# A decoder layer on one core: the order of loads, weights and first queries in the prologue

## The chip, the cores and the metric

One core of a Trainium2 chip. The metric is the device time of one execution in microseconds, the median of several. TensorE, VectorE, ScalarE and GpSimd each run their own instruction stream and wait for each other by semaphores; SP issues DMAs. All DMAs of the core run on its 16 DMA engines.

## The reference

One decoder layer over x of 4 x 512 tokens, 512 features, in float32:

```
x = x + attention(layernorm(x))        # norm again with g_norm, q = xn @ Wq (16 heads of 128),
                                       # k, v = xn @ Wkv (one head shared by all), q and k l2-normalised,
                                       # softmax(4 q . 4 k) @ v, @ Wout, layernorm with g_out
x = x + experts(layernorm(x), ids)     # silu(h @ Wg.T) * (h @ Wu.T) @ Wd.T, one of 4 experts by token id,
                                       # all three weights are ctx
x = x + bitlinear ffn(layernorm(x))    # weights rounded to -1, 0, 1, inputs to 8 bits, gelu between
```

## The kernel before, in words

Nearly every matrix product is done as three 16-bit products (`split_products`): each operand is a high part and a low part (the rest), and high x high, high x low and low x high are summed in PSUM. High parts are made by ScalarE, low parts by VectorE. A batch of x has four tiles of 128 tokens.

The prologue, batch 0:
- SP loads x 0, the norm weights `gn` (512 values spread over 128 partitions, four bytes each), x 1 to 3, Wkv (512 KB), the token ids `idi` (2048 four-byte pieces) and block 0 of Wq (1 MB, four heads; there are four blocks). Then `turn_x` transposes the four tiles by DMA, each after its low part (`x_lo`), and Wq blocks 1 and 2 and two pieces of Wout follow.
- VectorE waits for GpSimd's constants (`consts`), takes statistics (`input_stats`), normalises (`input_norm`), and makes low parts (`input_low`). GpSimd makes the power -0.5 (`input_rstd`). ScalarE makes high parts (`input_high`). `gws` is the norm weight times 64; it scales the rows of Wkv and Wq when their high and low parts are made (`query_weight`, per block and chunk of 128 features, one chunk 512 columns; `query_weight_high` is the high part on VectorE, used for block 1).
- TensorE runs 33 filler products (`busy_small`) once two low parts are there, then `keys_values` 0 and 1 (tiles 0, 1 and 2, 3: 24 products of 256 columns each), two small products for the routing of tokens to experts, query blocks 0 to 5, twelve fillers, and the loop over heads.
- A query block `queries(u)` is one tile of 128 tokens by four heads: 12 products of 512 columns. Its banks are `S` for u = 0 to 3, `QB` or `OUTB` after that. After it ScalarE takes squares (`query_squares`), GpSimd the power (`query_norm`), ScalarE the high part (`query_high`), VectorE the low part (`query_low`), and SP transposes the result (`turn_q`). Scores of heads 0 to 3 need all four blocks 0 to 3.
- VectorE does the routing (`routing_counts`, `routing_places`) between the weights of block 0 and the low parts of the keys.

The loop over 64 steps (four batches of 16 heads), step g on TensorE: `scores(g)` (12 products of 512 columns), `values(g - 1)` (48 products of 128 or 129 columns), from head 16 on `outputs`, and `queries(g + 6)`. ScalarE makes the exponentials of g in two halves, VectorE casts them and subtracts (`probabilities`); these low parts (`p_lo`) release `values(g)`. GpSimd turns a piece of Wout per step (`wout_parts`). In steps 11 and 12 the keys of the next batch are done too. Block 3 of Wq is turned into parts in steps 1 to 5, x of the next batch in steps 0 to 9.

The experts and the ffn follow; the change doesn't touch them.

## Time and profile before

| | |
|---|---|
| median of 3 runs | 955.84 us (954.51 to 956.09) |
| the profiled execution | 953.94 us |
| its span | 952.1 us, 19241 instructions |
| TensorE busy | 919.0 us, 97% |
| VectorE busy | 701.6 us, 74% |
| ScalarE busy | 616.5 us, 65% |
| GpSimd busy | 328.1 us, 34% |
| queue of SP (and ScalarE) | 117.25 MB, 56.2% of 16 DMA engines |

The span is the time on the device between the first and the last recorded instruction; the execution's own time has 1.8 us more around it. A busy TensorE is a row of products one behind the other: a product's own duration is longer than its distance to the next. Line numbers are those of the kernel before.

### The profile page before, as it was taken

Reading aid. Unit: us, or ns where it says so; the run is one execution under the profiler, and the core shown is the slowest. Engines: PE = TensorE matmul, PEld = TensorE weight load, DVE = VectorE, ACT = ScalarE, POOL = GpSimd, SP = SyncE. Lnnn points to the kernel's source line nnn. Section 1 sums busy time; section 2 is a strip of 40 time slices with the busy share of each in tenths; the row PEclk is TensorE's granted clock in tenths of the full one; section 3 lists DMA queues with packets and bytes.
Section 4 is the critical chain, followed back from the end, with each engine's and each line's share of the span. In section 5 each row is a group of like instructions: output and inputs, shape, how many; then the busy total and the mean of one; then the engine's idle time right before and its main releaser. Section 6 shows DMA issues by size and latency. Waiting matters only on the chain.

```text
span 952.1 us, 19241 instructions
## 1 busy us (share of the span) xinstructions
PE 919.0 (97%) x6635; PEld 522.8 (55%) x6635; DVE 701.6 (74%) x1540; ACT 616.5 (65%) x1573; POOL 328.1 (34%) x454
## 2 busy tenths in 40 slices
PE   4999999999999999999999999999997999999995
PEld 3466676655656556655666555656543444444442
DVE  6799978787786767787576766688564468877784
ACT  4877777767776756766667666765302269988672
POOL 4578867223332314323233313221141012322222
PEclk9999999999999999999999999999999999999998
DMA  9747547577867654554535444447985998544352
GB/s 243 176 90 136 122 101 119 137 196 170 211 167 156 156 135 110 112 134 112 127 81 120 100 112 101 116 106 177 206 210 134 192 191 166 119 96 97 86 135 73
DMA packets 303599, 131.60 MB, mean 138 GB/s; under 512 B 273168, under 2 KB 277776, under 8 KB 303504
## 3 DMA queue, kind: packets, MB, share of 16 engines
q1 hardware_dynamic: 299504, 117.25, 56.2%
q0 software_dynamic: 4000, 13.13, 3.9%
q8 instruction: 54, 0.88, 0.4%
q14 instruction: 41, 0.34, 0.1%
HBM read 42.76 MB, written 21.25 MB: 67 GB/s over the span
## 4 chain that ended last, share of the span: by engine, by line
PE 84%; DVE 5%; DMA 4%; ACT 2%; issue 2%; POOL 1%; SPq 1%; DVEq 0%; ACTq 0%; POOLq 0%
PE S L260 8%; PE S L258 8%; PE S L259 8%; PE O L635 6%; PE O L633 6%; PE O L637 6%; PE QB L258 6%; PE QB L259 6%; PE QB L260 6%; PE OUTB L259 5%; PE OUTB L258 5%; PE OUTB L260 5%; PE S L762 4%; PE OUTB L796 4%; DMA P<-QTOKR 2%
## 5 line engine op out<-in xcount | busy, mean ns | idle before, releaser
L633 PE MATMUL O<-V,P 128*128 128x129 f16 x1024 | 179.0, 219 | 1.6 <-DVE P L1255 1.4
L635 PE MATMUL O<-V,P 128*128 128x128 f16 x1024 | 179.1, 221 | 0.0
L637 PE MATMUL O<-V,P 128*128 128x129 f16 x1024 | 178.9, 218 | 0.0
L1253 DVE CAST P<-P 128x1024 bf16<-128x1024 f32 x128 | 93.2, 728 | 111.9 <-ACT P L915 111.8
L1255 DVE TENSOR_TENSOR P<-P 128x1024 f16<-128x1024 f32 x128 | 160.7, 1256 | 4.4
L915 ACT ACTIVATE P<-S,cst 128x1024 f32<-128x1024 f32 x128 | 142.5, 1114 | 29.1 <-PE S L260 27.4
L1609 POOL TENSOR_SCALAR qst<-qs 128x4 f32<-128x4 f32 x64 | 14.4, 225 | 344.1 <-ACT junk L898 344.1
L898 ACT ACTIVATE junk<-QB 128x128 bf16<-128x128 f32 x208 | 54.6, 277 | 102.1 <-PE QB L260 102.1
L926 ACT ACTIVATE OTOK<-O,rd 128x128 f16<-128x128 f32 x256 | 80.6, 376 | 43.1 <-DVE rd L1260 40.4
L633 PEld LDWEIGHTS O<-V,P 128*128 128x128 bf16 x1024 | 98.5, 96 | 9.7 <-DVE P L1255 2.5
L635 PEld LDWEIGHTS O<-V,P 128*128 128x128 bf16 x1024 | 99.2, 97 | 7.2
L637 PEld LDWEIGHTS O<-V,P 128*128 128x128 f16 x1024 | 100.8, 98 | 0.0
L258 PE MATMUL S<-XQA,KT 128*128 128x512 f16 x256 | 97.0, 379 | 0.3 <-DMA XQA<-P 0.3
L260 PE MATMUL S<-XQA,KT 128*128 128x512 f16 x256 | 97.0, 379 | 0.0
L259 PE MATMUL S<-XQA,KT 128*128 128x512 f16 x256 | 97.0, 379 | 0.0
L258 PE MATMUL QB<-WQA,XQA 128*128 128x512 f16 x208 | 78.8, 379 | 0.7 <-DVE QTOKR L1243 0.7
L259 PE MATMUL QB<-WQA,XQA 128*128 128x512 f16 x208 | 78.8, 379 | 0.0
L260 PE MATMUL QB<-WQA,XQA 128*128 128x512 f16 x208 | 78.8, 379 | 0.0
L1610 POOL TENSOR_TENSOR rn<-qst,half 128x4 f32<-128x4 f32 x64 | 71.3, 1115 | 5.3
L259 PE MATMUL OUTB<-WOA,OTA 128*128 128x512 f16 x192 | 72.8, 379 | 0.0
L260 PE MATMUL OUTB<-WOA,OTA 128*128 128x512 f16 x192 | 72.8, 379 | 0.0
L258 PE MATMUL OUTB<-WOA,OTA 128*128 128x512 f16 x192 | 72.7, 379 | 0.0
(260 smaller groups left out, 1983.9 us busy)
## 6 DMA issues: line engine op xcount, KB each, us to landing
SIDE<-in_L_ffn_w_dram SPq DMA_DIRECT2D x64, 256.0 KB, 2.8
OTA<-sorted_rows SPq DMA_DIRECT2D x4, 1028.0 KB, 7.1
OTA<-in_L_attn_Wq_dram SPq DMA_DIRECT2D x4, 1024.0 KB, 7.7
SIDE<-in_L_attn_Wout_dram SPq DMA_DIRECT2D x16, 256.0 KB, 3.0
SIDE<-in_ctx_dram SPq DMA_DIRECT2D x16, 256.0 KB
ctx_split<-SIDE SPq DMA_DIRECT2D x16, 256.0 KB
ROWB<-in_x_dram SPq DMA_DIRECT2D x16, 256.0 KB, 3.2
w_tern<-SIDE SPq DMA_DIRECT2D x32, 128.0 KB, 2.9
```

The source lines that it names most:

```text
L258: nc.tensor.matmul(o, lh, rh, start=first, stop=False)
L259: nc.tensor.matmul(o, lh, rl, start=False, stop=False)
L260: return nc.tensor.matmul(o, ll, rh, start=False, stop=last)
L633: nc.tensor.matmul(o, ph(g)[:, a:a + P], V[:, b % 2, j, 0:129], start=j == 0, stop=False)
L635: nc.tensor.matmul(o[:, 0:128], ph(g)[:, a:a + P], V[:, b % 2, j, 130:258], start=False, stop=False)
L637: last = nc.tensor.matmul(o, pl(g)[:, a:a + P], V[:, b % 2, j, 0:129], start=False, stop=j == NT - 1)
L898: last = nc.scalar.activation(junk[:, i * P:(i + 1) * P], qbank(u)[:, i * P:(i + 1) * P], ACT.Square, scale=16.0 / WS, accum_out=qs[:, u % ...
L915: nc.scalar.activation(P32[:, half * 1024:(half + 1) * 1024], S[:, half * 1024:(half + 1) * 1024], ACT.Exp, bias=off_p).then_inc(p_exp, 1)
L926: last = nc.scalar.activation(OTOK[:, g % 2, t * P:(t + 1) * P], o_tile(t), ACT.Copy, scale=rd[:, g % 2, t:t + 1])
L1253: nc.vector.tensor_copy(ph(g)[:, cols], P32[:, cols]).then_inc(p_hi, 1)
L1255: nc.vector.tensor_tensor(pl(g)[:, cols], P32[:, cols], ph(g)[:, cols], ALU.subtract).then_inc(p_lo, 1)
L1610: nc.gpsimd.tensor_tensor(rn[:, s, :], qst[:, s, :], half4[:, :], ALU.pow).then_inc(q_rn, 1)
```

## The change

It touches the prologue and the first steps.
- **Loads.** The four tiles of x go first, then the norm weights as one row into partition 0 of a buffer (`gn`), Wkv and Wq block 0. Wq block 1 is issued from ScalarE's queue after the last high part of x. The ids are loaded in step 8, the counts of the routing are taken in step 11, its two products are done in step 15, its places in step 16.
- **Norm weights.** Four products of the row with a single 1.0 turn it into four columns of `QB`, from which `gws` is made.
- **x and Wkv.** VectorE waits for the constants only before the weights of Wq. High and low parts of tile 2 and the norm of tile 3 come ahead of the parts of Wkv, which are released chunk by chunk.
- **Queries.** Blocks u = 0 to 3 are two heads by two tiles (24 products of 256 columns); scores of heads 0 and 1 wait for blocks 0 and 1 alone, heads 2 and 3 for 2 and 3. Blocks 0, 1, 4 and 5 have banks in `S` and `O`, 2 and 3 in `QB` and `OUTB`. Block 5 is done after scores 0.
- **Fillers.** 42 instead of 33 ahead of the keys, from the first high part of x on; none before scores 0.
- **Weights.** Wq block 2's high parts are made on VectorE, its last chunk in step 1; chunk 0 of block 1 on ScalarE.

The diff, cut to its core:

```diff
...
-gn = sb("gn", [P, DC], F32)
...
+gn = ROWB[0:1, 0, 0:D]
...
 def qtok(u):
-    return P32[:, u * 512:(u + 1) * 512].bitcast(F16) if u < 4 else QTOKR[:, u % 2, :]
+    if u < 4:
+        return P32[:, u * 512:(u + 1) * 512].bitcast(F16) if u < 2 else P16[:, (2 + u) * 1024:(3 + u) * 1024]
+    return QTOKR[:, u % 2, :]
...
 def qbank(u):
-    return S[:, u * 512:(u + 1) * 512] if u < 4 else OUTB[:, :] if u % 2 and u < 20 else QB[:, :]
+    if u in (0, 1, 4, 5):
+        return (S if u < 4 else O)[:, u % 4 * 512:(u % 4 + 1) * 512]
+    return OUTB[:, :] if u % 2 and u < 20 else QB[:, :]
...
 def kvbank(n):
...
+QT0 = QT[0].rearrange("p (q i s t h n) -> p q i s t h n", q=2, i=2, s=2, t=2, h=2)
...
 def wq_w(s, c, q):
...
+        if u < 4:
+            sp.dma_start_transpose(QT[0][:, u * 1024:(u + 1) * 1024].rearrange("p (a n) -> p a n", n=P),
+                                   qtok(u)).then_inc(qt[t], 16)
+            return
...
-    load_x(0)
-    sp.dma_start(gn[:, :], g_norm.rearrange("(c p) -> p c", p=P), allow_slow_non_contiguous=True
-                 ).then_inc(g_in, 16)
-    for k in range(1, NT):
-        load_x(k)
-    wkv_st = P16[:, 0:2048].bitcast(F32).rearrange("p (c n) -> p c n", c=DC)
-    sp.dma_start(wkv_st, Wkv.rearrange("(c p) n -> p c n", p=P)).then_inc(wkv_in, 16)
     def load_wq(q):
...
-    sp.dma_start(idi[:, :], ids.rearrange("b (t p) -> p (b t)", p=P),
-                 allow_slow_non_contiguous=True).then_inc(ids_in, 16)
+    for k in range(NT):
+        load_x(k)
+    sp.dma_start(gn, g_norm.rearrange("(a n) -> a n", a=1)).then_inc(g_in, 16)
+    sp.dma_start(P16[:, 0:2048].bitcast(F32).rearrange("p (c n) -> p c n", c=DC),
+                 Wkv.rearrange("(c p) n -> p c n", p=P)).then_inc(wkv_in, 16)
...
-    for q in range(1, 3):
-        load_wq(q)
+    load_wq(2)
...
-    turn_q(5)
...
     for g in range(STEPS):
...
-        if g >= 1 and g + 5 < STEPS:
+        if g == 8:
+            sp.dma_start(idi[:, :], ids.rearrange("b (t p) -> p (b t)", p=P),
+                         allow_slow_non_contiguous=True).then_inc(ids_in, 16)
+        if g + 5 < STEPS:
...
-            if n == 0:
-                pe.wait_ge(wkv_lo, 1)
...
+                if n == 0 and i == 0:
+                    pe.wait_ge(wkv_lo, c + 1)
...
     def queries(u):
...
+        if u < 4:
+            p, i = divmod(u, 2)
+            for tt in range(2):
+                a = (2 * i + tt) * P
+                for c in range(DC):
+                    lh = [XT[0][:, (s * DC + c) * N + a:(s * DC + c) * N + a + P] for s in range(2)]
+                    rh = [wq_w(s, c, 0)[:, p * 256:(p + 1) * 256] for s in range(2)]
+                    if u == 0 and tt == 0:
+                        pe.wait_ge(wq_lo, c + 1)
+                    last = split_products(qbank(u)[:, tt * 256:(tt + 1) * 256], lh[0], lh[1], rh[0], rh[1],
+                                          c == 0, c == DC - 1)
+            last.then_inc(q_ps, 1)
+            return
...
-        if 6 <= u < 20:
-            pe.wait_ge(q_lo, u - 1)
+        if u in (4, 5):
+            pe.wait_ge(k_lo, 2)
+            pe.wait_ge(v_lo, 2)
+        elif 6 <= u < 20:
+            pe.wait_ge(q_lo, u - 3 if u < 8 else u - 1)
...
         if h == 0:
...
-        if hh == 0:
+        if grp == 0 and hh % 2 == 0:
+            pe.wait_ge(qt[hh], 16)
+            pe.wait_ge(qt[hh + 1], 16)
+        elif hh == 0:
...
-            if g == 0:
-                pe.wait_ge(q_lo, 4)
-            else:
+            if g >= 1:
...
+            if grp == 0:
+                qr = [QT0[:, hh // 2, :, s, :, hh % 2, :] for s in range(2)]
+            else:
+                qr = [QT[grp % 2][:, (4 * s + hh) * N:(4 * s + hh + 1) * N] for s in range(2)]
...
-                    KT[:, b % 2, N + j * P:N + (j + 1) * P], QT[grp % 2][:, hh * N:(hh + 1) * N],
-                    QT[grp % 2][:, (4 + hh) * N:(5 + hh) * N], True, True)
+                    KT[:, b % 2, N + j * P:N + (j + 1) * P], qr[0], qr[1], True, True)
...
     def values(g):
...
-        if g == 0:
-            pe.wait_ge(k_lo, 2)
...
+            elif t % 2 == 0:
+                pe.wait_ge(q_lo, 5 + t // 2)
...
-            pe.wait_ge(q_lo, 20)
+            pe.wait_ge(pos_ready, 1)
...
-    pe.wait_ge(x_lo, 2)
-    busy_small(33)
+    pe.wait_ge(g_in, 16)
+    for c in range(DC):
+        last = nc.tensor.matmul(QB[:, c:c + 1], gn[:, c * P:(c + 1) * P], onesf[0:1, 0:1], start=True, stop=True)
+    last.then_inc(small_ps, 1)
+    pe.wait_ge(x_hi, 1)
+    busy_small(42)
...
-    pe.wait_ge(setup, 3)
-    nc.tensor.matmul(OUTB[:, 0:E * TILES], lower[:, :], scm[:, :], start=True, stop=True)
-    nc.tensor.matmul(OUTB[:, 64:64 + E * TILES], onesb[:, :], scm[:, :], start=True, stop=True
-                     ).then_inc(small_ps, 1)
     for u in range(5):
...
-    pe.wait_ge(pos_ready, 1)
-    queries(5)
-    pe.wait_ge(q_lo, 4)
-    for i in range(12):
-        nc.tensor.matmul(S[:, 0:512], onesb[:, :], wq_w(0, i % DC, 0), start=True, stop=True)
     for g in range(STEPS):
...
+        if g == 0:
+            queries(5)
...
+        if g == HEADS - 1:
+            pe.wait_ge(setup, 3)
+            pe.wait_ge(q_lo, 20)
+            nc.tensor.matmul(OUTB[:, 0:E * TILES], lower[:, :], scm[:, :], start=True, stop=True)
+            nc.tensor.matmul(OUTB[:, 64:64 + E * TILES], onesb[:, :], scm[:, :], start=True, stop=True
+                             ).then_inc(small_ps, 1)
...
+    def load_wq(q):
+        act.dma_start(OTA[:, q * 2048:(q + 1) * 2048].rearrange("p (c n) -> p c n", c=DC),
+                      Wq[:, q * 512:(q + 1) * 512].rearrange("(c p) n -> p c n", p=P)
+                      ).then_inc(wq_in[q], 16)
+    def key_value_weight(c):
+        nc.scalar.activation(WKV[:, c * 256:(c + 1) * 256],
+                             P16[:, 0:2048].bitcast(F32)[:, c * 256:(c + 1) * 256], ACT.Copy,
+                             scale=gws[:, c:c + 1]).then_inc(wkv_hi, 1)
...
-    for k in range(NT):
+    for k in range(3):
...
-        if k == 1:
-            act.wait_ge(wkv_in, 16)
-            act.wait_ge(setup, 1)
-            for c in range(DC):
-                last = nc.scalar.activation(
-                    WKV[:, c * 256:(c + 1) * 256],
-                    P16[:, 0:2048].bitcast(F32)[:, c * 256:(c + 1) * 256], ACT.Copy,
-                    scale=gws[:, c:c + 1])
-            last.then_inc(wkv_hi, 1)
+    act.wait_ge(wkv_in, 16)
+    act.wait_ge(setup, 1)
+    for c in range(DC):
+        key_value_weight(c)
+    input_high(3)
+    load_wq(1)
...
-    key_squares(1)
...
+    key_squares(1)
+    query_weight(1, 0)
+    value_high(1)
...
-    value_high(1)
...
-    query_squares(5)
-    query_high(4)
-    query_high(5)
-    for c in range(DC):
-        query_weight(2, c)
...
     for g in range(STEPS):
...
-        if g >= 1 and g + 5 < STEPS:
+        if g == 0:
+            query_high(4)
+            query_squares(5)
+        if g + 5 < STEPS:
...
     def routing_places():
...
-        dve.wait_ge(small_ps, 1)
+        dve.wait_ge(small_ps, 2)
...
     def query_weight(q, c):
-        if q != 1:
-            dve.wait_ge(wq_hi, DC * (q - (q > 1)) + c + 1)
+        if q in (0, 3) or (q == 1 and c == 0):
+            dve.wait_ge(wq_hi, (0, DC, 0, DC + 1)[q] + c + 1)
...
+        elif g == 1:
+            dve.wait_ge(qt[2], 16)
+            dve.wait_ge(qt[3], 16)
...
     def weight_scales_set():
-        dve.wait_ge(small_ps, 2)
+        dve.wait_ge(small_ps, 3)
...
-    dve.wait_ge(consts, 1)
...
-    dve.wait_ge(g_in, 16)
-    nc.vector.tensor_scalar(gws[:, :], gn[:, :], WS, None, ALU.mult).then_inc(setup, 1)
+    dve.wait_ge(small_ps, 1)
+    nc.vector.tensor_scalar(gws[:, :], QB[:, 0:DC], WS, None, ALU.mult).then_inc(setup, 1)
...
-    dve.wait_ge(wkv_hi, 1)
+    input_low(2)
+    input_norm(3)
...
-        last = weight_low(WKV[:, (DC + c) * 256:(DC + c + 1) * 256],
-                          P16[:, 0:2048].bitcast(F32)[:, c * 256:(c + 1) * 256],
-                          WKV[:, c * 256:(c + 1) * 256], c)
-    last.then_inc(wkv_lo, 1)
-    input_norm(3)
-    input_low(2)
+        dve.wait_ge(wkv_hi, c + 1)
+        weight_low(WKV[:, (DC + c) * 256:(DC + c + 1) * 256],
+                   P16[:, 0:2048].bitcast(F32)[:, c * 256:(c + 1) * 256],
+                   WKV[:, c * 256:(c + 1) * 256], c).then_inc(wkv_lo, 1)
...
+    dve.wait_ge(consts, 1)
...
-    routing_counts()
-    routing_places()
-    for n in range(2):
-        key_low(n)
-        value_low(n)
-    for c in range(DC):
+    key_low(0)
+    value_low(0)
+    query_weight_high(1, 1)
+    query_weight(1, 1)
+    query_weight(1, 0)
+    key_low(1)
+    value_low(1)
+    for c in range(2, DC):
...
-    for c in range(DC):
...
-    for u in range(6):
+    query_weight_high(2, 0)
+    query_weight(2, 0)
+    query_low(0)
+    query_low(1)
+    for u in range(2, NT):
+        query_weight_high(2, u - 1)
+        query_weight(2, u - 1)
...
-    for c in range(DC):
-        query_weight(2, c)
...
     for g in range(STEPS):
...
+        if g == HEADS:
+            routing_places()
...
+        if g == 0:
+            query_low(4)
+            query_low(5)
...
+        if g == 1:
+            query_weight_high(2, 3)
+            query_weight(2, 3)
...
+        if g == HEADS - 5:
+            routing_counts()
...
-    for u in range(6):
+    for u in range(5):
...
+    wout_parts(0)
     for g in range(STEPS):
-        if g >= 1 and g + 5 < STEPS:
+        if g + 5 < STEPS:
...
-        if g < HEADS:
+        if 1 <= g < HEADS:
...
```

## Rows read from the trace of the kernel before

**Rows 1.** Waits of TensorE from 60 us to the end: total us, times, longest.

```profile
PE O L732 <- issue: 4.2, 2, 4.0
```

**Rows 2.** TensorE in order of time, single rows: start us, us, what, idle before.

```profile
10.91 3.50 PE L674 MATMUL OUTB<-onesb,lower 128*128 128x128 bf16 x33 [10.91 <-DVE P L1218]
...
15.35 0.28 PE L258 MATMUL O<-WKV,XQA 128*128 128x256 f16 x1 [0.94 <-DMA XQA<-P]
...
17.25 0.28 PE L258 MATMUL O<-WKV,XQA 128*128 128x256 f16 x1 [0.41 <-DMA XQA<-P]
...
21.24 0.38 PE L258 MATMUL S<-WQA,XQA 128*128 128x512 f16 x1
...
36.85 2.76 PE L696 MATMUL S<-WQA,onesb 128*128 128x512 f16 x12
...
39.89 0.38 PE L258 MATMUL S<-XQA,KT 128*128 128x512 f16 x1 [0.27 <-DMA XQA<-P]
...
49.23 0.23 PE L633 MATMUL O<-V,P 128*128 128x129 f16 x1 [1.41 <-DVE P L1255]
...
80.94 0.22 PE L633 MATMUL O<-V,P 128*128 128x129 f16 x1
```

**Rows 3.** Busy time by engine in two stretches; last DMA share, GB/s.

```profile
4.00:8.00 4.00, 0.00 (x0) 0.00 (x0) 3.17 (x8) 0.63 (x1) 2.10 (x7) 1.00 1.00 285
8.00:9.00 1.00, 0.00 (x0) 0.00 (x0) 1.00 (x4) 0.73 (x2) 0.92 (x2) 1.00 0.70 10
```

**Rows 4.** SP's issues in order of time: start us, us.

```profile
4.25 4.09 SPq L420 DMA_DIRECT2D OTA<-in_L_attn_Wq_dram  x1
...
8.94 8.00 SPq L326 DMA_TRANSPOSE XQA<-P  x4
```

**Rows 5.** ScalarE in order of time.

```profile
14.30 2.56 ACT L843 ACTIVATE WQA<-OTA,gws 128x512 f16<-128x512 f32 x4 [0.83 <-DMA OTA<-in_L_attn_Wq_dram]
...
26.62 0.28 ACT L898 ACTIVATE junk<-S 128x128 bf16<-128x128 f32 x1 [1.45 <-PE S L260]
```

**Rows 6.** Transposes of x by line, up to 25 us.

```profile
DMA to landing us min/median/max: 6.4/6.4/6.4
```

**Rows 7.** Transposes of queries by line, up to 60 us.

```profile
DMA to landing us min/median/max: 2.7/2.8/5.3
```

**Rows 8.** VectorE in order of time.

```profile
4.40 0.69 DVE L1208 BATCH_NORM_STATS2 st<-P 128x6 f32<-128x512 f32 x1 [4.40 <-POOL OS L1584]
...
8.23 0.68 DVE L1218 TENSOR_TENSOR P<-P 128x512 f16<-128x512 f32 x1
...
10.68 1.67 DVE L1191 SCALAR_TENSOR_TENSOR WKV<-P,gws,WKV 128x256 f16<-128x256 f32 x4
...
12.72 1.47 DVE L1218 TENSOR_TENSOR P<-P 128x512 f16<-128x512 f32 x2
...
25.27 2.04 DVE L1195 TENSOR_SCALAR WQA<-OTA,gws 128x512 f16<-128x512 f32 x4
27.35 2.74 DVE L1191 SCALAR_TENSOR_TENSOR WQA<-OTA,gws,WQA 128x512 f16<-128x512 f32 x4
30.00 2.15 DVE L1243 SCALAR_TENSOR_TENSOR P<-S,rn,P 128x128 f16<-128x128 f32 x8
...
77.87 1.51 DVE L1255 TENSOR_TENSOR P<-P 128x1024 f16<-128x1024 f32 x1
...
174.25 0.69 DVE L1253 CAST P<-P 128x1024 bf16<-128x1024 f32 x1 [1.94 <-ACT P L915]
```

**Rows 9.** GpSimd in order of time, Wout part 0.

```profile
39.47 1.52 POOL L1615 TENSOR_SCALAR SIDE<-SIDE 128x512 f32<-128x512 f32 x1
...
41.76 1.16 POOL L1617 TENSOR_TENSOR WOA<-SIDE,WOA 128x512 f16<-128x512 f32 x1
```

**Rows 10.** Busy time by engine from values 1 to values 3, by head.

```profile
57.16:65.09 7.93, 7.93 (x73) 5.10 (x72) 7.51 (x16) 6.15 (x20) 7.52 (x8) 1.00 0.51 132
65.09:73.02 7.93, 7.93 (x74) 5.10 (x72) 7.86 (x17) 6.67 (x21) 5.01 (x6) 1.00 0.75 102
```

## The prediction

> **What bounds the kernel.** I read the page first, then TensorE's waits, then the order of time on each engine over the first 90 us. The page has TensorE busy for 97% of the span. After 60 us its waits fall into eight groups; the largest is 4.2 us in two waits [rows 1], in the stage of the experts. So from the first values on TensorE is back to back, and whatever brings that point forward or back shifts the whole rest with it. The prologue is therefore read as one question: when do the values of head 0 begin? Before, at 49.23 [rows 2].
>
> What lies ahead of 49.23 [rows 2]: the first keys and values product at 15.35, held by the turned x; 33 filler products before it (10.91 to 14.41); tile 1 at 17.25, also held by its transpose; keys and values done at 21.2; six query blocks (72 products, 21.24 to 36.8, 0.216 us each); twelve filler products and a wait up to 39.89; scores 0, queries 6, scores 1 (12 products each, 2.59 us, so up to 47.65); then to 49.23 a wait for the probabilities. Real work from 21.2 to 49.23 is 15.55 + 3 x 2.59 = 23.3 us; the other 4.7 us are fillers and waits.
>
> **Part 1: loads and x.** DMA runs full early: 285 GB/s from 4 to 8 us, but 10 GB/s at 0.70 busy from 8 to 9 [rows 3], which is the token ids with their four-byte pieces. SP stood 4.09 us in the issue of the first Wq block [rows 4], it landed at 14.3 (ScalarE's wait, [rows 5]), and the transposes of x, queued behind it, took 6.4 us to land [rows 6] where those of q take 2.7 to 2.8 [rows 7]. The change takes the ids out, makes the norm weights one row and keeps the order x, Wkv, Wq block 0. That is 2.62 MB; at 285 GB/s from about 2.0 us it is through at 11.2, landed 11.5. The first transpose lands 1.1 behind it, as before (14.3 to 15.35 less the start): 12.6. The second comes 1.9 later as before (15.35 to 17.25): 14.5.
>
> VectorE no longer waits for GpSimd's constants, which held it to 4.40 [rows 8]; x 0 had landed by then, and x 1, which held the next statistics, is issued one DMA earlier. I give both 0.4 us (bounds 0 and 0.8). So low part 0 goes from 8.91 to 8.5. The norm weights now come by four products of one row. They need g_in, which stands behind all of x, about 6.8, and the products, for which I have no row; four one-column products cannot take less than nothing, and 1.2 us is four of the slowest filler products (0.31 each) as a bound. VectorE wants them at 7.9, so 0 to 0.4 us late; I take 0.1. Then low 2 is moved ahead of the Wkv low parts: 11.1 instead of about 13.4. The Wkv high parts start after high 2 on ScalarE, near 10.5; the low parts (1.67, [rows 8]), each behind its high part, go from 11.5 to 13.2 instead of to 12.3. Low 3 then ends at 13.9 (before 14.19: 12.72 + 1.47). SP is free at that time (before, its own stall had the four issues last to 16.94, [rows 4]), so transpose 3 is issued at 13.9 and lands between 2.8 [rows 7] and 6.4 us [rows 6] later; I take 3.5, since Wq block 0 is through but block 1 has just been issued from ScalarE, at 12.8: 17.4. TensorE: tile 0 from 12.6, its last chunk held by the Wkv low part to 13.2, tiles 1 and 2 at 14.5 and 15.9, tile 3 at 17.4 to 18.7. **Keys and values end at 18.7, 2.5 us earlier** (bounds: tile 3 landing at 16.7 gives 3.2, at 20.3 it gives -0.4).
>
> The block from ScalarE's queue is the place to weigh a rule. The rows show the DMA engines at their limit until 18 us, and one queue's transposes stuck behind its own 1 MB load. The Trainium skill (DMA: Bandwidth & Descriptors, Issuing engines are not separate DMA queues) says that DMAs started by different engines run on the same 16 engines and interleave. By that, block 1 takes half the rate from transpose 3 instead of waiting behind it, and lands at the 6.4 end; were the queue its own path, 2.8 would hold. The 3.5 above does not hang on it.
>
> **Part 2: from keys to the first scores.** Queries 0 to 3 become two heads by two tiles: 24 products of 256 columns instead of 12 of 512. The keys and values products are of that form, 36 of them from 17.25 to 21.2 [rows 2], 0.109 us; 96 x 0.109 = 10.5 against 48 x 0.216 = 10.4, +0.1. Scores 0 now need only the transposes of query blocks 0 and 1, and query block 5 is done after scores 0. Before, query block 1's squares began at 26.62 [rows 5] and its low part ended at 32.15 [rows 8], 5.5 us. After: query block 1 is done at 18.7 + 5.2 = 23.9; squares at 24.1, low part at 29.4 to 29.6, its transpose lands 2.8 later, 32.3. TensorE has done five query blocks by 18.7 + 13.1 = 31.8. So scores 0 wait 0.5 us. Ahead on VectorE now stand weights of Wq blocks 1 and 2, 0.51 + 0.68 = 1.2 us a chunk [rows 8], five chunks before low part 0, plus the key and value low parts. From Wq block 1 landing (about 20) that is 20 + 1.9 + 0.9 + 3.6 = 26.4, where query block 0's high part is ready at 26.2. There is 1.5 us of room here, since query block 1's low part waits for its high part (28.0) anyway; Wq block 1 may land up to about 21.8. The bounds of the wait are 0 and 2.9 us (Wq block 1 landing near 23, the 10 us that block 0 took from its issue at 4.25 to 14.3, and scores 0 that much later).
>
> Wq block 2's high parts move from ScalarE (2.6 us) to VectorE; that is hidden behind ScalarE's squares. The order after that: scores 0 32.3, queries 5, queries 6, scores 1, values 0 at 32.3 + 4 x 2.59 = **42.7**. Needed by then: probabilities 0 low, done near 39 (exponentials 33.8 to 36.0, four VectorE passes of 3.8 us in all), and the low part of queries 5, whose banks the values take: queries 5 end 37.5, squares 1.1, GpSimd to 40.2 (it has Wout part 0 ahead, 3.4 us, first and last of three steps in [rows 9], from about 35.4), high 1.1, low 1.1: 42.4. It holds only the second half of values 0, at 44.0. So the 1.6 us wait of before goes, with little room. The fillers go for nothing.
>
> **Part 3: what is put later.** VectorE carries in head 1 one more weight chunk, 1.2 to 1.4 us. There it was busy for 7.51 of 7.93 us, and 7.86 in the next heads [rows 10], so nearly as full as TensorE. The room before values 4 was 1.6 us: low part done at 79.38 [rows 8], values at 80.94 [rows 2]. In the new order VectorE enters head 1 about 0.8 us later against the values (ScalarE has high 5 and squares 6 before the exponentials), plus 1.3 less 0.4 of idle: 1.7 against 1.6, and the same for the chunk that queries 8 want. I take **0.7 us lost** (bounds 0 and 3). The ids (head 8), the counts (head 11) and the places (head 16) fall into steps where VectorE has room (TensorE has keys in head 11 and outputs from head 16 besides; ahead of the first pass of head 16 VectorE idled 1.94 us, [rows 8]): nothing. They are 9 and 8 small linked steps, about 2 us each, and if that cover were gone they would cost that once.
>
> **Sum.** 2.5 + (49.23 - 21.2 - 23.3 - 0.1 - 0.5) = 2.5 + 4.1 = 6.6, less 0.7: 5.9 us. On the profiled execution that is 953.94 - 5.9 = 948.0. It was 1.9 us below the median of the three runs, 955.84; from that median 949.9.
>
> **Rivals.**
> *(a) A late link in the middle.* Wq block 1 or transpose 3 lands late. For: DMA is full and both share it. Against: without the ids some 1 us of DMA time is back. Each 1 us past 21.8 or 17.4 costs 1 us: with 2.5 us lost, 952.4.
> *(b) Nothing comes earlier in front:* transposes stay 6.4 us behind, keys and values end at 21.2; only part 2 stays, 4.1 - 0.7 = 3.4 us: 952.4. Here the change doesn't do what its first part says.
> *(c) VectorE becomes the bound over heads 1 to 6.* This is the one that ends on the other side: it was at 7.86 of 7.93 us a head; at 9.0 us a head over six heads the 6.6 us are gone, at 9.3 it is 957.4. For: no room from head 3. Against: the added work is one chunk, and the low parts come 7.9 to 8.4 apart now.
> *(d) The clock.* 128-column fillers started 0.106 us apart while the 256-column ones after them took 0.109 [rows 2]: the first stretch ran at the 1.2 GHz level, the second at 2.4, although the granted clock is printed 1.00 [rows 3]. TensorE had been idle until 10.91. Now 42 fillers run from about 7.3 to 11.8, gaps of 0.8, 0.5 and 0.5 us follow. The 1.6 us gap before values 0 cost no clock, so I expect none. If scores 0 waited near 3 us at the same time as the clock fell, some 3.5 us of products would run at half rate, 1.8 us more: 951.7 and up. The Trainium skill (TensorE: Matmul & The Clock Gate, HAM oscillation) warns of just such idle gaps between bursts, and the fillers that covered this wait are gone.
> *(e) More than forecast:* transpose 3 lands 2.8 after its issue, no wait for scores 0, VectorE keeps up: 3.2 + 4.6 = 7.8 us, 948.0.
>
> **From this to numbers.** Forecast as told (5 to 7 us gained) 0.46; (e) 0.14; (a) 0.15; (b) 0.10; (c) 0.10, of which 0.04 slower than before; (d) 0.05. The range takes in (e) and (a), (b): 947.3 to 953.8; the likeliest alone is 948.8 to 951.0. Faster by over 0.2% (1.9 us, about what a measurement of this kernel can tell from no change) 0.85, within it 0.09, slower 0.06.
>
> **What will show it.** Right: first keys product near 12.6, last near 18.7; no fillers before scores 0, which start near 32.3 on their transpose; values 0 near 42.7; from there the same rows shifted by 6. Each term wrong: transposes of x still 6 us to landing; Wq block 1 after 22; a wait of values 1 to 5 or queries 8 on VectorE; filler or keys products at half rate. The prediction as a whole fails if values 0 begin after 47, or if TensorE's waits after 60 us grow by several us.

## The result, and the profile after

The changed kernel takes 962.75 us (median of four executions, 960.74 to 964.9), before beside it 955.17: a ratio of 1.0078, interval 1.0054 to 1.0102. Timed again with ten executions (c1 below) it is 960.38 us, 1.0053, interval 1.0032 to 1.0073. So it is 5 to 7.5 us **slower**, where 5.9 us faster was forecast. The profiled execution took 961.4 us, span 959.7.

TensorE after, in order of time, the rows that answer to [rows 2]:

```profile
6.00 1.84 PE L712 MATMUL QB<-onesf,ROWB 1*128 1x1 f32 x8 [6.00 <-DMA ROWB<-in_L_attn_g_norm_dram]
7.77 3.85 PE L701 MATMUL OUTB<-onesb,lower 128*128 128x128 bf16 x42
12.44 0.28 PE L265 MATMUL O<-WKV,XQA 128*128 128x256 f16 x1 [0.82 <-DMA XQA<-P]
...
16.95 0.28 PE L265 MATMUL O<-WKV,XQA 128*128 128x256 f16 x1 [3.03 <-DMA XQA<-P]
...
21.09 0.39 PE L265 MATMUL O<-WKV,XQA 128*128 128x256 f16 x1 [1.82 <-DMA XQA<-P]
...
23.19 0.42 PE L266 MATMUL O<-WKV,XQA 128*128 128x256 f16 x1
23.41 0.42 PE L267 MATMUL O<-WKV,XQA 128*128 128x256 f16 x1
...
25.25 0.27 PE L265 MATMUL S<-WQA,XQA 128*128 128x256 f16 x1
...
38.68 0.38 PE L265 MATMUL S<-XQA,KT 128*128 128x512 f16 x1 [0.20 <-DMA XQA<-P]
...
49.04 0.22 PE L660 MATMUL O<-V,P 128*128 128x129 f16 x1
...
58.59 0.22 PE L660 MATMUL O<-V,P 128*128 128x129 f16 x1 [0.57 <-DVE OTOK L1306]
...
99.89 0.22 PE L660 MATMUL O<-V,P 128*128 128x129 f16 x1 [0.22 <-DVE OTOK L1306]
```

And three of TensorE's waits over the whole span (total us, times, longest), which answer to [rows 1]:

```profile
PE O L265 <- DMA XQA<-P: 5.7, 3, 3.0
PE S L843 <- DMA XQA<-sorted_h: 4.4, 1, 4.4
PE OUTB L265 <- DMA P<-QTOKR: 2.9, 2, 2.0
```

The reader is to see three places. (1) The first keys product comes at 12.44, almost as forecast (12.6), but the next tiles are at 16.95 and 21.09, and the keys and values end at 25.25: 4.0 us later than before, where 2.5 us earlier was forecast. (2) From there to values 0 (49.04) it is 23.8 us, forecast 24.0, before 28.0: part 2 of the change does what it should. (3) Values 6 come at 99.89, 50.85 us behind values 0. Before it was 47.57 (49.23 to 96.80), a head each 7.93 us. Values 1 alone are 9.55 us behind values 0. From values 6 to the last head's values, step 63, all kernels of this study take the same 575.14 us, and the last stage then takes 284.7 us, 280.2 before.

SP and ScalarE's queue in the prologue, in order of time, and in a second view the landing of the transposes of x (SP's rows answer to [rows 4], the landing to [rows 6]):

```profile
3.50 0.50 SPq L423 DMA_DIRECT2D OTA<-in_L_attn_Wq_dram  x1
8.66 9.33 SPq L333 DMA_TRANSPOSE XQA<-P  x4
18.03 0.58 SPq L423 DMA_DIRECT2D OTA<-in_L_attn_Wq_dram  x1
...
11.77 0.41 ACTq L1006 DMA_DIRECT2D OTA<-in_L_attn_Wq_dram  x1
```

```profile
DMA to landing us min/median/max: 3.7/7.2/9.3
```

SP no longer stalls in the issue of Wq block 0 (0.50 against 4.09 us). But all four transposes are in flight or not yet issued when ScalarE issues the 1 MB block 1 at 11.77, and they take up to 9.3 us to land. The four landed at 12.39, 16.90, 21.04 and 21.96. (They are counted from one here; the prediction and the recorded expectations count from zero, so their transpose 3 is the fourth. Tiles are counted from zero throughout.)

What the DMA queues moved from 16 to 19 us (packets, MB, share of the 16 engines; q1 is SP's queue, q10 is ScalarE's, which a1's trace doesn't have):

```profile
q10 hardware_dynamic: 382, 0.78, 84.6%
q1 hardware_dynamic: 381, 0.10, 14.5%
```

Here the two queues take turns about packet for packet. A packet of the block is 2 KB, one of the transposes 256 bytes, so the block gets eight times the bytes. With nothing beside them (c2, 11 to 14 us) the transposes' queue moved 2183 packets in three microseconds. c1 shows nearly the same (381 and 358); in a3, c4 and d2 SP's queue got fewer still in this stretch (174, 233 and 87 against 400, 363 and 439). From 13 to 16 us, while GpSimd's load of `g_out` ran too, SP's queue moved 41 packets, against 1064 in a1, where only `g_out` is beside it. The 16 engines were not at their limit in those three microseconds of after (a share of 0.54 to 0.85, 86 to 152 GB/s); why they moved so little isn't shown.

Windows of the stretch (the last three columns are granted clock, DMA share, GB/s):

```profile
15.00:17.00 2.00, 0.05 (x1) 0.05 (x2) 1.56 (x3) 0.11 (x1) 0.00 (x0) 1.00 0.87 198
17.00:21.00 4.00, 2.27 (x12) 1.34 (x12) 0.00 (x0) 0.63 (x4) 0.89 (x2) 0.55 1.13 286
21.00:25.00 4.00, 3.91 (x22) 2.91 (x23) 2.09 (x5) 0.90 (x3) 0.02 (x1) 0.59 1.08 380
25.00:29.00 4.00, 4.00 (x39) 3.59 (x38) 1.93 (x5) 3.07 (x16) 0.88 (x2) 1.00 0.10 37
```

After the idle 3.03 us TensorE's granted clock is 0.55, mostly its 1.2 GHz level, and the products of tiles 2 and 3 stand 0.21 us apart instead of 0.11 (23.19, 23.41 above) until 24.26. Tile 2 landed at 21.04 and tile 3 at 21.96, while TensorE was still busy with tile 2. At 0.109 us each the 24 products that begin at 21.09 would end at 23.7 instead of 25.25. So of the 4.0 us late the landings hold 2.5 and the clock 1.5.

GpSimd and ScalarE in head 0 after:

```profile
42.66 1.75 POOL L1669 TENSOR_SCALAR SIDE<-SIDE 128x512 f32<-128x512 f32 x1
44.48 0.61 POOL L1670 CAST WOA<-SIDE 128x512 f16<-128x512 f32 x1
45.17 1.47 POOL L1671 TENSOR_TENSOR WOA<-SIDE,WOA 128x512 f16<-128x512 f32 x1
46.62 1.16 POOL L1663 TENSOR_SCALAR qst<-qs 128x4 f32<-128x4 f32 x1
47.87 1.03 POOL L1664 TENSOR_TENSOR rn<-qst,half 128x4 f32<-128x4 f32 x1
...
48.93 1.14 ACT L938 ACTIVATE QTOKR<-O,rn 128x128 f16<-128x128 f32 x4 [3.54 <-POOL rn L1664]
```

Query block 5 now comes behind scores 0, so its power on GpSimd has Wout part 0 before it. ScalarE's in-order stream waits for that power with the exponentials of head 1 behind it. They begin at 50.95, and values 1 pay for it.

### The profile page after: what moved, and what is told of

It reads as the page before. It is cut to its first block, busy times and chain, and to the rows that moved or that the text cites. A ratio compares the mean times of both kernels' runs of the same rounds, so it can differ in the third digit from the quotient of the medians.

```text
span 959.7 us, 19346 instructions
## 1 busy us (share of the span) xinstructions
PE 925.3 (96%) x6688; PEld 530.3 (55%) x6688; DVE 705.4 (74%) x1543; ACT 614.4 (64%) x1570; POOL 328.0 (34%) x454
## 4 chain that ended last, share of the span: by engine, by line
PE 71%; DVE 8%; DMA 5%; SPq 4%; issue 3%; ACT 3%; POOL 2%; DVEq 0%; ACTq 0%; POOLq 0%
PE S L267 5%; PE S L266 5%; PE S L265 5%; PE O L662 5%; PE O L660 5%; PE O L664 5%; PE QB L265 5%; PE QB L267 5%; PE QB L266 5%; PE OUTB L267 4%; PE OUTB L266 4%; PE OUTB L265 4%; PE S L793 4%; PE OUTB L827 4%; SPq L478 2%
## 5 line engine op out<-in xcount | busy, mean ns | idle before, releaser
L946 ACT ACTIVATE P<-S,cst 128x1024 f32<-128x1024 f32 x128 | 142.5, 1120 | 23.4 <-PE S L267 23.1
L265 PE MATMUL QB<-WQA,XQA 128*128 128x512 f16 (+1 forms) x212 | 79.5, 375 | 0.6 <-DVE QTOKR L1280 0.6
L266 PE MATMUL QB<-WQA,XQA 128*128 128x512 f16 (+1 forms) x212 | 79.5, 375 | 0.0
L267 PE MATMUL QB<-WQA,XQA 128*128 128x512 f16 (+1 forms) x212 | 79.5, 375 | 0.0
```

The lines of the kernel that those rows point to most:

```text
L265: nc.tensor.matmul(o, lh, rh, start=first, stop=False)
L266: nc.tensor.matmul(o, lh, rl, start=False, stop=False)
L267: return nc.tensor.matmul(o, ll, rh, start=False, stop=last)
L946: nc.scalar.activation(P32[:, half * 1024:(half + 1) * 1024], S[:, half * 1024:(half + 1) * 1024], ACT.Exp, bias=off_p).then_inc(p_exp, 1)
```

## The experiments

"Keys end" is the start of the first query product, "values 6" that of head 6 (from the profile of each run), "last stage" the time from the values of step 63 to the end of the span. These four are from one profiled execution each; the ratio is from all executions. Times of each group of runs are compared with executions of before on the same chip.

| run | keys end | values 0 | values 6 | last stage | ratio to before, interval |
|---|---|---|---|---|---|
| before | 21.24 | 49.23 | 96.80 | 280.2 | |
| after | 25.25 | 49.04 | 99.89 | 284.7 | 1.0078, 1.0054 to 1.0102 |
| a1 | 19.69 | 43.90 | 94.44 | 279.5 | 0.9970, 0.9949 to 0.9991 |
| a2 | 24.93 | 48.76 | 100.29 | 283.7 | 1.0049, 1.0031 to 1.0067 |
| a3 | 25.27 | 49.04 | 99.93 | 282.7 | one run, 959.49 us |
| a4 | 23.06 | 47.20 | 96.66 | 283.7 | one run, 957.23 us |
| b1 | 20.48 | 48.41 | 95.98 | 281.6 | 0.9990, 0.9975 to 1.0006 |
| b2 | 19.09 | 43.34 | 92.85 | 284.6 | 0.9967, 0.9948 to 0.9985 |
| b6 | 19.98 | 44.59 | 92.15 | 283.5 | 0.9957, 0.9938 to 0.9975 |
| b5 | 18.68 | 42.35 | 93.17 | 286.2 | one run, 956.23 us |
| c1 (after again) | 25.42 | 49.24 | 100.09 | 282.6 | 1.0053, 1.0032 to 1.0073 |
| c4 | 25.99 | 49.76 | 100.59 | 283.6 | 1.0044, 1.0021 to 1.0067 |
| c2 | 17.94 | 42.65 | 90.21 | 281.5 | 0.9965, 0.9947 to 0.9983 |
| c3 | 19.68 | 43.11 | 92.59 | 282.6 | 0.9964, 0.9949 to 0.9979 |
| d1 | 22.59 | 46.38 | 97.26 | 284.7 | 1.0005, 0.9982 to 1.0029 |
| d2 | 25.12 | 53.12 | 100.69 | 282.4 | 1.0034, 1.0011 to 1.0057 |
| d3 (before again) | 20.57 | 48.56 | 96.13 | 280.5 | one run, 954.78 us |

### a1: Wq block 1 on SP, behind the transposes of x

```diff
 # ScalarE, behind the high part of x 3
-load_wq(1)
 # SP, behind the transposes of x
+load_wq(1)
 load_wq(2)
```

> The changed kernel with Wq block 1 issued by SP behind the four transposes of x instead of from ScalarE's queue. Theory Q (block 1's 1 MB, issued from ScalarE at 11.8, shares the DMA engines with the transposes of x and holds tiles 1 to 3 back): transpose 1 lands near 14.5 instead of 16.9, transposes 2 and 3 by 18, so keys and values end at 19 to 20 instead of 25.3, with no fall of the clock. Block 1 itself lands later (about 24 instead of 20.5) and holds VectorE's chain, so scores 0 start at 34 to 37 instead of 38.7; the total falls by 2 to 4 us. Rival R (transposes of x are slow by themselves or held by the load of g_out from GpSimd): keys and values still end after 24 and the total stays within 1 us.

Three views of a1: SP's rows, the landing of the transposes, and two windows.

```profile
9.11 6.60 SPq L333 DMA_TRANSPOSE XQA<-P  x4
15.76 1.21 SPq L423 DMA_DIRECT2D OTA<-in_L_attn_Wq_dram  x2
```

```profile
DMA to landing us min/median/max: 2.8/3.7/4.5
```

```profile
15.00:17.00 2.00, 1.48 (x12) 1.09 (x12) 2.00 (x4) 0.57 (x1) 0.00 (x0) 1.00 1.07 206
17.00:21.00 4.00, 3.95 (x38) 3.55 (x38) 0.96 (x4) 2.15 (x11) 1.23 (x4) 1.00 0.97 277
```

The landing view counts only the transposes of which it has every record, here the first two of four. The trace also holds the 16 updates by which each transpose reports its landing, and these give all four (us from issue to landing):

| run | first | second | third | fourth |
|---|---|---|---|---|
| before | 6.4 | 6.4 | 3.6 | 3.1 |
| after | 3.7 | 6.4 | 9.3 | 8.0 |
| a1 | 2.8 | 4.5 | 4.8 | 3.6 |
| b6 | 2.8 | 4.1 | 4.4 | 3.1 |
| c2 | 3.2 | 2.8 | 2.8 | 2.7 |
| d1 | 5.1 | 6.9 | 5.5 | 7.7 |
| d2 | 5.6 | 8.1 | 7.5 | 7.0 |

In all seven traces in which ScalarE issued the block between 11.4 and 13.6 us (after, a2, a3, a4, c1, c4, d2) the third transpose landed 0.6 to 0.9 us behind the block itself.

This one edit brings the keys' end from 25.25 to 19.69, the clock stays up, and the kernel passes from slower to faster than before. It is the main cause of the loss, shown. By the ratios the total falls by 8 us (from c1's 1.0053), twice what was expected; the front explains 5.6 of it. Heads 1 to 6 still lose: values 6 are 50.54 us behind values 0.

### a2: Wout part 0 behind the power of query block 5

```diff
 for u in range(5):
     query_norm(u)
-wout_parts(0)
...
-    if 1 <= g < HEADS:
+    if g < HEADS:
         wout_parts(g)
```

> The changed kernel with Wout part 0 on GpSimd put back behind the power of query block 5. Theory G (GpSimd's 3.9 us of Wout part 0 delays the power of block 5, ScalarE stands from 45.3 to 48.9 behind it and the exponentials of head 1 come 1.9 us late, which is where heads 1 to 6 fall behind): the exponentials of head 1 start near 49.0 instead of 50.95, values 6 follow values 0 by 48 to 49.3 us instead of 50.85 (47.57 in the kernel before), the total falls by 1.5 to 2.5 us. Rival V (VectorE simply has more work than TensorE in heads 1 to 6): values 6 less values 0 stays above 50.3.

The exponentials of head 1 came at 49.10 instead of 50.95, but part 0 then delayed the power of block 6 (done at 53.17), and values 6 came 51.53 us behind values 0, 0.7 more than in after. That is the number of rival V, but not its cause: the work was only pushed one place on, and b6 takes it out of the way.

### a3: fillers between the tiles of x

```diff
+if n == 0 and i == 0:
+    busy_small(48)
...
 keys_values(0)
+busy_small(30)
 keys_values(1)
```

> The changed kernel with 48 filler products after tile 0 of keys 0 and 30 between keys 0 and keys 1; they lie in TensorE's waits for the transposes. Theory C (the clock fell at 17.4 because TensorE had stood idle for 3 us): the 24 products of keys 1 take 2.6 us instead of 4.16, granted clock 1.00 throughout, scores 0 begin 1.5 us earlier, near 37.2. Rival: the fall has nothing to do with the idle time, keys 1 still take near 4.2 us, and the fillers only add work.

The granted clock was 1.00 in every window from 8 to 30 us, and the 24 products of keys 1 took 2.63 us (22.64 to 25.27) instead of 4.16: theory C holds, and the clock's 1.5 us in after is shown. Still the keys ended at 25.27, as without fillers, because the third transpose landed at 22.59 here, 1.5 us later. Why it did (block 1 itself landed 1.4 us later, at 21.89) isn't shown, nor that fillers would bring a gain.

### a4: the last chunk of Wq block 2 in head 0

```diff
 query_low(4)
+query_weight_high(2, 3)
+query_weight(2, 3)
 query_low(5)
...
-if g == 1:
-    query_weight_high(2, 3)
-    query_weight(2, 3)
```

> The changed kernel with the last chunk of Wq block 2 on VectorE taken from head 1 into the wait before the low part of query block 5. Theory V (VectorE has too much work in heads 1 to 6): values 6 less values 0 falls by the chunk's 1.2 us, to 49.6. Theory G (heads are late because ScalarE's exponentials of head 1 are): VectorE merely idles elsewhere in head 1, and it falls by under 0.5 us; to a part both can hold, since VectorE is at 7.86 of 7.93 us a head.

Values 6 came 49.46 us behind values 0 instead of 50.85, and from values 1 on every head took 7.93 us. The keys' end also moved here, by 2.2 us, which this edit has no part in. The third transpose landed 0.7 us earlier than in after (20.38), and the clock was at its full level when tiles 2 and 3 came (their 24 products took 2.6 us): the landings of the prologue vary between executions of after's kind, and the clock with them. The time is one run.

### b1: the kernel before, its norm weights issued by ScalarE

```diff
-sp.dma_start(gn[:, :], g_norm.rearrange("(c p) -> p c", p=P), ...)   # SP, behind x 0
+act.dma_start(gn[:, :], g_norm.rearrange("(c p) -> p c", p=P), ...)  # ScalarE, first
```

> The kernel before, with one edit: the 2 KB load of the norm weights is issued by ScalarE instead of SP. Nothing else changes, and it is the only transfer on ScalarE's DMA queue. The three kernels that used that queue (after and two experiments) spent 282.7 to 284.7 us from the last head's values to the end, the two that did not 279.5 and 280.2. Theory D (using a second hardware DMA queue at all makes the experts' stage slower): 283 to 284.5 us from the last values to the end, profiled span 2 to 4 us above before's 952.1, ratio 1.003 to 1.005. Rival S (the stage at the end varies by some us from run to run or with the timing of its loads, and the queue is not its cause): 279 to 281.5 us, ratio 0.999 to 1.001, or a tail that differs without the time of the whole following. In both, keys and values end within 0.5 us of 21.2.

Theory D fell. A small transfer on ScalarE's queue alone makes nothing slower: the last stage is 281.6 us, where D wanted 283 or more, and the ratio is 0.999.

### b2: a1 and a4 together

> After, with Wq block 1 loaded by SP behind the transposes of x (as in a1) and the fourth chunk of Wq block 2 made in head 0 by VectorE between the low parts of queries 4 and 5 (as in a4), not in head 1. Theory V (that chunk sits on VectorE's path in heads 1 to 5): values 0 within 0.6 us of a1's 43.9 and values 6 about 49.3 to 49.8 us behind them, where a1 had 50.5: 1 us under a1, ratio to before 0.995 to 0.997. Rival P (in head 1 it fills idle time, and what VectorE loses is set by ScalarE's late exponentials of head 1): values 6 again 50.3 to 50.7 us behind values 0, ratio as a1's 0.997 or, with the chunk ahead of the low part of queries 5, 0.998.

Values 6 49.51 us behind values 0, a1 50.54: theory V holds for 1.0 us of the trace; the ratio, 0.9967, can't be told from a1's.

### b6: b2, and all Wout parts one head later

```diff
-wout_parts(0)                       # GpSimd, ahead of the loop
...
-    if 1 <= g < HEADS:
-        wout_parts(g)
+    if 1 <= g <= HEADS:
+        wout_parts(g - 1)
...
-    if b == 0 and 1 <= h < HEADS - 1:   # SP
-        load_wout(h + 1)
+    if b == 0 and 2 <= h:
+        load_wout(h)
```

> The edits of b2 and one more: every part of Wout is made by GpSimd one head later (part h in head h + 1, behind the power of the query block of that head), its loads by SP one head later too. In a1 ScalarE idled 3.4 us at 40 to 43.5 us for the power of query block 5, because GpSimd had Wout part 0 before it. Theory G2 (that wait delays the exponentials of head 1 and so values 1): ScalarE's wait falls to under 1.5 us, the exponentials of head 1 begin at 43.5 or earlier instead of 45.5, values 1 come 8.0 to 8.5 us behind values 0 instead of 9.3, values 6 48.0 to 48.8 us behind values 0, and the time is 1 to 1.5 us under b2's: ratio to before 0.993 to 0.995. Rival V2 (VectorE is full from head 0 on whatever order GpSimd has): the exponentials come earlier, yet values 6 stay 49.3 or more behind values 0, and the time equals b2's within 0.4 us.

ScalarE's wait for the power of block 5 fell from 3.42 us (a1) to 1.82, a little above what was expected, and all heads take 7.93 us: values 6 are 47.56 us behind values 0, before's own 47.57. From the keys' end to values 6 it is 72.2 us, against 73.8 in b2, 74.6 in after and 75.6 before. Theory G2 holds in the trace and V2 fell. The time doesn't show it: 952.41 us against b2's 952.71, and a ratio of 0.9957 where G2 wanted 0.993 to 0.995. The loss in heads 1 to 6 is thus explained whole in the trace, by the Wout parts (2.0 us) and the chunk (1.0 us, 1.4 in a4).

### b5: a1, the row of norm weights from ScalarE

```diff
-sp.dma_start(gn, g_norm.rearrange("(a n) -> a n", a=1)).then_inc(g_in, 16)   # SP
+act.dma_start(gn, g_norm.rearrange("(a n) -> a n", a=1)).then_inc(g_in, 16)  # ScalarE, first
```

> After with Wq block 1 on SP (as in a1), and the 2 KB row of norm weights issued by ScalarE instead of SP; the only transfer on ScalarE's queue. Theory D: 283 us or more from the last values to the end (a1: 279.5). Rival S: 279 to 281.5. Theory Q (what cost the front was the 1 MB block ahead of the transposes, not the second queue): keys and values end within 0.5 us of a1's 19.7 and the granted clock stays at 1.00 up to 26 us; the row lands earlier than 5.5 us, so the scaled weights are ready before VectorE asks, up to 0.5 us earlier in front.

Keys ended at 18.68, 1.0 us before a1 and so a little earlier than theory Q said, at a clock of 1.00. The last stage of 286.2 is what theory D said, but b2, which has nothing on that queue, has 284.6, so it is no support for it.

### c1: after, again

> The changed kernel itself, unedited, timed again beside before. Its trace had values 6 3.1 us later than before's, and 4.5 us more from the last values to the end; the time was 7.5 us more, from four executions. [...] Theory K (the change itself costs the last stage 4 us): ratio 1.007 to 1.009 and a last stage of 284 us or more. [...]

The front is the same within 0.2 us. The last stage is 2.1 us shorter than in the first profile, so two executions of one kernel differ by that much there. K's lower bounds, 284 us and 1.007, are not met. But see d3.

### c4 and d1: the block from ScalarE, later

```diff
 input_high(3)
-load_wq(1)
 for c in range(DC):
     query_weight(0, c)
+act.wait_ge(wq_hi, DC)     # d1 alone
+load_wq(1)
```

> After, with one edit: ScalarE issues Wq block 1 behind its four high parts of Wq block 0, at about 15.1 us, instead of ahead of them at 11.8. The block stays on ScalarE's queue. The last transposes of x are issued by about 14 us. Theory O (what costs is that 1 MB is in flight at the same time as the transposes, whichever queue it came by): the transposes land 3 to 4.5 us after their issue as in a1, keys and values end at 19.5 to 21, the clock stays above 0.9, values 0 at 44 to 45.5, ratio 0.996 to 1.001. Rival Q2 (a second hardware queue makes transposes slow by itself, or one MB issued at 15 still catches the fourth one): transpose 4 lands 6 us or more behind its issue, keys and values end after 23, ratio as after's.

> After, with Wq block 1 issued by ScalarE behind its four high parts of Wq block 0 and behind a wait for them, so that the issue can't run ahead of them (in the run before this one it did: it stood at 12.22 us although it was written behind activations that began at 13.0). It should now come at about 15.5 us, where SP issued it in a1 (15.76). The transposes of x are then all issued (by 13.9 to 14.4). Theory O (what costs is the megabyte being in flight together with the transposes of x): they land in 4.5 us at most, as in a1, keys and values end at 19.5 to 21 and the clock stays above 0.9 to 25 us; values 6 at 94.4 to 96, ratio 0.996 to 1.000. Rival Q2 (a block on a second queue slows the transposes even when it is issued behind them): the fourth still takes 6 us or more, keys and values end after 23, ratio 1.003 or more.

ScalarE's rows of c4:

```profile
10.90 1.69 ACT L1011 ACTIVATE WKV<-P,gws 128x256 f16<-128x256 f32 x4
12.22 0.41 ACTq L1006 DMA_DIRECT2D OTA<-in_L_attn_Wq_dram  x1
12.50 0.61 ACT L882 ACTIVATE P<-P 128x512 f16<-128x512 f32 x1
13.02 2.54 ACT L874 ACTIVATE WQA<-OTA,gws 128x512 f16<-128x512 f32 x4
```

c4 was no test: the issue, written behind the activations of 12.50 and 13.02, started before them, since nothing made it wait for them; all else is as in after. d1 has the wait; ScalarE's row and the landing in d1:

```profile
14.89 0.41 ACTq L1006 DMA_DIRECT2D OTA<-in_L_attn_Wq_dram  x1
```

```profile
DMA to landing us min/median/max: 5.1/6.0/6.9
```

This view again has only the first two. The fourth transpose, issued at 13.49, took 7.7 us, as rival Q2 said (6 or more), where it took 3.6 in a1. In both the block was issued 1.4 us behind it. From 18 to 20 us ScalarE's queue moved 350 packets and SP's 5. So the second queue holds the transposes back even when its load is issued behind them. The rest of Q2 missed, and O too: the keys end at 22.59, 2.7 us before after and 2.9 behind a1, and the ratio is 1.0005. Issuing the block 3.1 us later on the same queue gives half of the loss back. The clock has 1.5 us of that, since it stayed at 1.00 here, where TensorE's longest wait was 2.2 us. The other half goes with the other queue, though d1's first two transposes, which landed at 13.29 and 16.95, were also slower than a1's, in part ahead of the block.

### d2: that edit alone, on the kernel before

```diff
 # SP
-for q in range(1, 3):
-    load_wq(q)
+load_wq(2)
 # ScalarE, behind the four high parts of x
+load_wq(1)
```

> The kernel before with one edit of the change alone: Wq block 1 is issued by ScalarE behind its high part of x 3 (at about 12.8 us) instead of by SP behind the transposes of x. Theory O/Q: the transposes of x, which took 6.4 us in the median before, take 8 to 11, keys and values end at 24 to 26 instead of 21.2, with the clock at its lower level for some us; the twelve fillers and the wait before scores 0 (3.1 us) take up part of it, since Wq block 1 lands earlier than the 25 us of before: values 0 at 50 to 53, ratio 1.001 to 1.004. Rival (in before's order, where SP's queue already has Wq block 0 ahead of the transposes, nothing more is lost): keys and values end within 1 us of 21.2 and the ratio is 0.997 to 1.001.

Keys end at 25.12 instead of 21.24 (20.57 in d3), the clock is at 0.73 from 20 to 25 us, values 0 come at 53.12, and the ratio is 1.0034. The transposes took 5.6 to 8.1 us, less than expected. The move of the block alone makes the kernel before slower, by 3.9 to 4.6 us of front; in the changed kernel it was 5.6.

### c2: b6, and the load of g_out in head 10

```diff
-nc.gpsimd.dma_start(GO[:, :], g_out.partition_broadcast(P)).then_inc(go_in, 16)   # prologue
...
+    if g == 10:
+        nc.gpsimd.dma_start(GO[:, :], g_out.partition_broadcast(P)).then_inc(go_in, 16)
```

> The edits of b6 (Wq block 1 on SP, the chunk in head 0, Wout parts one head later) and one more: the 256 KB load of g_out, which GpSimd issued at about 11 us while the transposes of x were under way, is issued by GpSimd in head 10. Theory L (it shares the DMA engines with the transposes of x): tiles 1 and 3 of x land 0.3 to 0.8 us earlier, TensorE's waits of b6 for them (1.8 us in two) fall to 1.2 or less, keys and values end that much closer to the first transpose, ratio 0.3 to 0.8 thousandths under b6's, which the timing alone can't tell from none. Rival: the transposes of one tile follow 1.3 to 1.9 us behind another whatever else is in flight: the same waits as in b6.

Landing of the transposes of x, and TensorE's rows of c2:

```profile
DMA to landing us min/median/max: 2.7/2.8/3.2
```

```profile
17.94 0.27 PE L265 MATMUL S<-WQA,XQA 128*128 128x256 f16 x1
...
42.65 0.22 PE L661 MATMUL O<-V,P 128*128 128x129 f16 x1
...
50.58 0.22 PE L661 MATMUL O<-V,P 128*128 128x129 f16 x1
...
90.21 0.22 PE L661 MATMUL O<-V,P 128*128 128x129 f16 x1
```

Theory L holds in the trace: with GpSimd's 256 KB out of the way too, the four transposes land in 3.2 us at most (b6: 4.4), TensorE waits for them 0.2 us after the first tile instead of 0.8, and the keys take 5.8 us from the first product instead of 6.6. Of the 2.0 us by which the keys end before b6's, 1.2 come from an earlier first product. Values 0 at 42.65 is the forecast's 42.7. The profiled execution took 948.6 us, the median of twelve is 950.99, and its ratio, 0.9965, is not below b6's. The load of `g_out` was not moved in a kernel with the block on ScalarE's queue, so its share in after's late landings is open.

### c3: b6 with query block 5 ahead of scores 0

```diff
-for u in range(5):
+for u in range(6):
     queries(u)
...
-    if g == 0:
-        queries(5)
```

> The edits of b6, and query block 5 put back ahead of scores 0 (one move of the change undone). TensorE waited 1.0 us before scores 0 in b6 and did query block 5 behind them. Theory W (scores 0 at 34.2 were held by their transposes; values 0 start when the products ahead of them are done): scores 0 begin at 35.7 to 36, straight after query block 5 and without a wait, and values 0 at 43.6 plus what the probabilities of head 0 are late; these need some 8 us from scores 0, so values 0 wait up to 0.5 us and begin at 43.6 to 44.2, 0.4 to 1 us earlier than b6's 44.6. Rival X (the chain from scores 0 over exponentials and probabilities sets values 0, and the move brought its 1.6 us whole): values 0 at 46 or later.

Scores 0 began at 35.34, values 0 at 43.11, 23.4 us behind the keys' end (24.6 in b6): theory W, a little more than it said. But head 1 then waited again (values 1 at 52.96), and values 6 are 72.9 us behind the keys' end, b6 72.2. This move of the change is worth 0.7 us of the trace and nothing that the times can tell.

### d3: before, again

> The kernel before itself, for a second profile: how far the last stage varies from one execution to the next. Theory T (scatter): from the last head's values to the end it takes another time than the 280.2 us of the first profile, by 1 us or more either way, with everything up to 110 us within 1 us of the first. Rival: 279.7 to 280.7, and then what the changed kernels show there, 281.5 to 284.7, would be theirs.

The front was 0.7 us earlier, and the last stage was 280.5 us: it didn't move by over 1 us, as T had it. Two profiles don't bound it, though. Before's 19 timed executions of this group range from 952.2 to 960.2 us.

## Why the prediction was wrong, by its own steps

- **The step that failed** is the price of the transposes of x beside Wq block 1: "so transpose 3 is issued at 13.9 and lands between 2.8 [rows 7] and 6.4 us [rows 6] later; I take 3.5", and, ahead of it, the third transpose, which got no term at all (its tile was taken as ready at 15.9). Counted from one, the second landed at 16.90 (14.5 forecast), the third took 9.3 us and landed at 21.04, and the fourth took 8.0 us and landed at 21.96 (17.4 forecast). The keys ended at 25.25 instead of 18.7. Wq block 0 was through at 11.38, as forecast. What held the transposes was block 1 on the second queue, packet for packet until it had landed at 20.48, and GpSimd's load of g_out. 6.4 was not the worst case but the landing behind block 0 on the same queue, and only of the first two; before's last two took 3.6 and 3.1. The sentence on the Trainium skill (DMA: Bandwidth & Descriptors, Issuing engines are not separate DMA queues) pointed the right way, and the trace agrees that the two queues interleave on the same engines (382 and 381 packets in 3 us). That the block would take "half the rate" was wrong: the transposes got half of the packets, which was a ninth of the bytes. This is 6.5 of the 9.0 us by which values 6 missed: 5.0 for the landings and 1.5 for the clock that fell behind them. Without the block and g_out (c2) the forecast's own 18.7 is met and passed, 17.94.
- **The clock, rival (d).** "The 1.6 us gap before values 0 cost no clock, so I expect none": the gap came elsewhere and was 3.03 us, and the clock was at half speed from 17.4 to 24.3. It cost 1.5 us, by the sum above and by a3. The Trainium skill (TensorE: Matmul & The Clock Gate, HAM oscillation) warns of gaps between bursts; the trace agrees, with 0.55 granted. (The reading "the granted clock is printed 1.00 [rows 3]" names rows that end at 9 us, ahead of the fillers; the trace of before prints 1.00 from 10 to 16 us as well.)
- **Part 1, the rest.** x 0's statistics came at 3.39 (4.0 forecast), low 0 was done at 8.63 (8.5), lows 0 to 3 by 13.9 (13.9), and the first product came at 12.44 (12.6): right. The row's products were 1.84 us, where 1.2 was given as a bound from the fillers: eight records at 6.00 to 7.84, in float32. VectorE waited 0.52 us for them, 0.1 was taken.
- **Part 2** was right term by term: keys' end to scores 0 13.4 us (13.6), scores 0 to values 0 10.36 (10.4). Scores 0 waited 0.2 (0.5). The second half of values 0 waited 0.7 us for block 5's low part, which was forecast as the tight place.
- **Part 3** was mis-sized: "0.7 us lost (bounds 0 and 3)" measured 3.3. The chunk on VectorE, which was all that this term priced, was 1.0 to 1.4 of it. The other 2.0 us were in the text, "it has Wout part 0 ahead, 3.4 us", but followed only to values 0 and not to what stands behind the waiting instruction on ScalarE: the exponentials of head 1. This is rival (c)'s place, by another engine.
- **"From there the same rows shifted".** True for 575.14 us from values 6 on, in every kernel. Not true for the last stage of the profiled executions: 284.7 and 282.6 us in after, 280.2 and 280.5 before.
- **The sum.** The forecast's 5.9 us, less 5.0 for the landings, 1.5 for the clock and 2.6 for part 3, plus 0.2 for part 2, makes values 6 3.0 us late (measured 3.1: 99.89 against 96.80). With 4.5 us of last stage it is the 7.5 us between the two profiled executions.
- **The rivals.** Rival (a) named the late link. By its own price, 1 us for each us past 17.4, the fourth transpose at 21.96 leaves 1.3 us of gain, so it would still have said faster: it had neither the third transpose, nor the clock, nor the exponentials of head 1.

**What stays open** is the last stage. In after VectorE waits there for the scatter of a row tile, which it didn't in either profile of before:

```profile
717.91 0.43 DVE L1349 CAST HR<-OS 128x512 f16<-128x512 f32 x1 [2.66 <-DMA sorted_h<-HR,posu]
```

Such waits of 0.2 to 3.0 us stand in all the edited kernels; TensorE's wait for the turned rows is then 2.1 to 4.6 us, where it is 0.9 to 1.2 in both profiles of before and in b1, and the clock falls as well (0.73 to 0.90 from 720 to 730 us in all of them but a1, b1 and c2, 1.00 in before). In after the clock is the larger part: TensorE idles 10.5 us in the last stage against 9.5 in before, and the granted clock of 0.87, 0.96 and 0.83 in 720 to 730, 730 to 740 and 760 to 770 us is 3.4 us of full speed lost. With the 1.0 us of idle time that is the difference. The edits of the study don't sort it: 279.5 with block 1 on SP, 284.6 with one chunk moved besides, 282.4 in d2, whose only edit is in the prologue. That a small shift of SP's and GpSimd's DMAs against each other does it is argued, not shown. A second buffer for that tile, which would show it, wasn't tried.

It may be less than the profiles say, for each of them is one execution. By the ratios, eleven edited kernels can be compared with the shift of their values 6: in nine of them the time moved with it within -0.6 and +1.2 us (with an uncertainty of 1.4 to 2.3 us each), though their profiled last stages were up to 4.5 us longer than before's. d1 has 284.7 and loses nothing by its ratio beyond the 0.5 us of its front. c1 has 1.8 us more than its front, the first timing of after 4.4, and c2, whose values 6 come 6.6 us earlier, gains only 3.3 us of time. Where c2 lost the rest isn't shown: its last stage was 1.3 us longer.
